# Attention and mixture of experts on one core: VectorE takes the lower halves of the expert weights, in four pieces per matrix

## The reference, cut to what matters

```python
scores_t = jnp.swapaxes(scores, 1, 2)
gate_vals, sel_idx = jax.lax.top_k(scores_t, capacity)        # capacity = 129
tokens = x[b_idx, sel_idx]
h = jnp.einsum('becd,edh->bech', tokens, w1) + b1[None, :, None, :]
h = jax.nn.gelu(h, approximate=False)
y = jnp.einsum('bech,ehd->becd', h, w2) + b2[None, :, None, :]
gated = y * gate_vals[..., None]
out = jnp.zeros_like(x).at[b_idx, sel_idx].add(gated)
```

## Time and profile before

| | us |
|---|---|
| median of 3 runs | 969.57 (967.61 to 969.59) |
| the profiled execution | 968.14 |
| its span, first to last instruction | 966.2 |
| TensorE busy with products | 833.6 (86% of the span) |
| VectorE, ScalarE, GpSimd busy | 649.0, 534.6, 527.7 |
| mean granted TensorE clock | 0.936 of full speed |

### The profile page before, as it was taken

The page is one execution under the profiler, slowest core; times in us unless marked ns, Lnnn a source line. Parts: engine busy times, 40 slices in busy tenths (PEclk is TensorE's granted clock), DMA queues, the critical chain, the costliest instruction groups (busy, mean ns, idle before and its releaser), DMA issues. The chain is left out here.

```text
span 966.2 us, 17052 instructions
## 1 busy us (share of the span) xinstructions
PE 833.6 (86%) x5864; PEld 623.9 (65%) x5864; DVE 649.0 (67%) x1985; ACT 534.6 (55%) x1042; POOL 527.7 (55%) x639
## 2 busy tenths in 40 slices
PE   4669999999999999977656899998989899898990
PEld 3434454544545453433356889998989899898990
DVE  4467778787877878999749955555464735547454
ACT  2126667667676766645345345564555556455455
POOL 6336665656565653323645247757375645738343
PEclk9768999999999999988879899999999999999995
DMA  4998778877776869100151324325242332422257
GB/s 142 165 151 134 123 121 144 144 144 143 141 147 112 153 99 205 62 24 20 47 202 53 74 40 82 96 38 137 35 126 45 93 63 47 125 34 35 37 132 250
DMA packets 90101, 100.51 MB, mean 104 GB/s; under 512 B 8736, under 2 KB 83488, under 8 KB 89888
## 3 DMA queue, kind: packets, MB, share of 16 engines
q1 hardware_dynamic: 72560, 77.92, 38.3%
q0 software_dynamic: 12800, 16.92, 10.3%
q10 hardware_dynamic: 4656, 4.59, 1.4%
HBM read 65.38 MB, written 33.62 MB: 102 GB/s over the span
## 5 line engine op out<-in xcount | busy, mean ns | idle before, releaser
L522 DVE CUSTOM_DVE_ANT_0 n_ps<-n_ps,tri 128x512 f32<-128x512 f32 (+3 forms) x512 | 238.8, 519 | 86.0 <-PE n_ps L652 84.3
L438 ACT ACTIVATE pt<-st_ps 128x512 f32<-128x512 f32 x320 | 184.3, 602 | 68.4 <-PE st_ps L637 53.2
L1090 DVE TENSOR_TENSOR h_lo<-g,h_hi 128x384 fp32r<-128x384 f32 (+1 forms) x184 | 132.6, 729 | 125.5 <-ACT h_hi L1026 116.3
L1166 PE MATMUL y_ps<-w_parts,h_hi 128*128 128x256 f32 (+1 forms) x1152 | 212.4, 279 | 0.3 <-ACT h_hi L1026 0.3
L1021 ACT ACTIVATE g<-h_ps,b 128x384 f32<-128x384 f32 (+1 forms) x192 | 104.3, 543 | 193.5 <-PE h_ps L1152 159.3
L1152 PE MATMUL h_ps<-tt_hi,w_parts 128*128 128x384 f32 (+1 forms) x768 | 177.3, 335 | 30.6 <-issue 20.0
L381 POOL TENSOR_SCALAR_AFFINE_SELECT pt<-pt 128x256 f32<-128x256 f32 (+1 forms) x320 | 110.7, 363 | 125.3 <-ACT pt L438 124.5
L1166 PEld LDWEIGHTS y_ps<-w_parts,h_hi 128*128 128x128 f32 (+1 forms) x1152 | 171.6, 177 | 3.6 <-ACT h_hi L1026 0.6
L993 POOL DMA_INDIRECT acc<-y,tok_no x64 | 103.7, 1621 | 114.7 <-DVE y L1104 105.9
L1166 PE MATMUL y_ps<-w_parts,h_lo 128*128 128x256 f32 (+1 forms) x576 | 160.6, 279 | 0.0
L1152 PEld LDWEIGHTS h_ps<-tt_hi,w_parts 128*128 128x128 f32 x768 | 132.2, 198 | 33.4 <-issue 31.8
(11 more groups left out here) (160 smaller groups left out, 1137.6 us busy)
## 6 DMA issues: line engine op xcount, KB each, us to landing
w_parts<-part_d SPq DMA_DIRECT2D x192, 128.0 KB, 6.5
w_raw<-in_w SPq DMA_DIRECT2D x16, 1024.0 KB
part_d<-w_raw SPq DMA_DIRECT2D x96, 128.0 KB, 6.6
w_raw<-in_xt SPq DMA_DIRECT2D x8, 512.0 KB, 4.7
res<-in_x SPq DMA_DIRECT2D x8, 512.0 KB, 10.4
x<-res SPq DMA_DIRECT2D x8, 512.0 KB, 3.3
acc<-res SPq DMA_DIRECT2D x8, 512.0 KB, 4.7
fin<-acc SPq DMA_DIRECT2D x4, 512.0 KB, 4.2
```

Source lines behind the costliest of these rows:

```text
L438: nc.scalar.activation(pt[:, slot % PT_RING, n % UP, :], st_ps[at % ST_RING][:, :], ACT.Exp, scale=S_SCALE).then_inc(exp_done, 1)
L522: ins = nc.vector.tensor_tensor_reduce(out=src[:, h, :], in0=src[:, h, :], in1=mask, scale=-1.0, scalar=-BIG_NEG, op0=ALU.add, op1=ALU.min ...
L1090: nc.vector.tensor_tensor(h_lo[:, q % 2, n, 0:cols], g[:, at % G_RING, 0:cols], h_hi[:, q % 2, n, 0:cols].bitcast(F32), ALU.subtract).then ...
L1166: ins = nc.tensor.matmul(y_ps[at % Y_RING][0:rows, 0:C], x[:, q % 2, m, toks], w[e % 2][:, m, :], start=i == 0, stop=i == len(terms) - 1)
```

## The change

In `experts`, GpSimd no longer makes the lower halves. VectorE makes each in four operations of 128 x 512, one per place of the order ("low1" and "low2", `low_at`): for experts 2 to 7 those of w1 at m = 3 to 6 of the pass of the cut, those of w2 at m = 7, 8, 9 and m = 0 of the next pass; for expert 1 those of w1 at m = 5 to 8 of pass 0, those of w2 at m = 9 of pass 0 and m = 0 to 2 of pass 1. A piece comes last at its place, behind "up", "turn" and "down". In `attention`, GpSimd still makes expert 0's, in four operations back to back. `w1_cut` and `w2_cut` count four per expert, and SyncE issues the next load at the stage of the fourth piece. ScalarE's part is as before.

```diff
@@ attention, gpsimd, stage "cut"
-                nc.gpsimd.tensor_tensor(lo, ahead[("w1_raw", "w2_raw")[n]][:, :, :], hi.bitcast(F32), ALU.subtract).then_inc(ahead[("w1_cut", "w2_cut")[n]], 1)
+                name, raw, cut = ("w1", "w2")[n], ahead[("w1_raw", "w2_raw")[n]], ahead[("w1_cut", "w2_cut")[n]]
+                for piece in range(PIECES):
+                    nc.gpsimd.tensor_tensor(piece_of(lo, name, piece), piece_of(raw, name, piece),
+                                            piece_of(hi, name, piece).bitcast(F32), ALU.subtract).then_inc(cut, 1)
@@
+PIECES = 4
@@
+def low_at(stage, e, piece):
+
+    q, m = cut_at("cut1" if stage == "low1" else "cut2", e)
+    m += (2 if stage == "low1" else 3 if e > 1 else 5) + piece
+    return q + m // (KH + 2), m % (KH + 2)
+
+
+def piece_of(part, name, piece):
+
+    if name == "w1":
+        return part[:, piece * KC // PIECES, (piece % 2) * HID // 2:(piece % 2 + 1) * HID // 2]
+    return part[:, piece * KH // PIECES:(piece + 1) * KH // PIECES, :]
@@ expert_steps, last at each place
+            for e in range(1, E):
+                for stage in ("low1", "low2"):
+                    for piece in range(PIECES):
+                        if (q, m) == low_at(stage, e, piece):
+                            yield stage, e, piece
@@ experts, sync
-            sp.wait_ge(w1_cut, e)
+            sp.wait_ge(w1_cut, PIECES * e)
...
-            if stage == "cut1" and q + 1 < E:
+            if stage == "low1" and n == PIECES - 1 and q + 1 < E:
                 load_w1(q + 1)
-            elif stage == "cut2" and q + 1 < E:
+            elif stage == "low2" and n == PIECES - 1 and q + 1 < E:
                 load_w2(q + 1)
@@ experts, gpsimd
-            elif stage in ("cut1", "cut2"):
-                raw, hi, lo, top, done = ((w1_raw, w1_hi, w1_lo, w1_top, w1_cut) if stage == "cut1" else
-                                          (w2_raw, w2_hi, w2_lo, w2_top, w2_cut))
-                pool.wait_ge(top, q + 1)
-                nc.gpsimd.tensor_tensor(lo[q % 2], raw[:, :, :], hi[q % 2].bitcast(F32), ALU.subtract).then_inc(done, 1)
@@ experts, vector
+            elif stage in ("low1", "low2"):
+                name, raw, hi, lo, top, done = (("w1", w1_raw, w1_hi, w1_lo, w1_top, w1_cut) if stage == "low1" else
+                                                ("w2", w2_raw, w2_hi, w2_lo, w2_top, w2_cut))
+                dve.wait_ge(top, q + 1)
+                nc.vector.tensor_tensor(piece_of(lo[q % 2], name, n), piece_of(raw, name, n),
+                                        piece_of(hi[q % 2], name, n).bitcast(F32), ALU.subtract).then_inc(done, 1)
@@ experts, tensor ("up" and, with w2_cut, "down")
-                    pe.wait_ge(w1_cut, e + 1)
+                    pe.wait_ge(w1_cut, PIECES * (e + 1))
```

More of the change, by code:

```diff
@@ L917, in load_w1 @@
         def load_w1(e):
-            sp.wait_ge(w1_cut, e)
+            sp.wait_ge(w1_cut, PIECES * e)
             sp.dma_start(w1_raw[:, :, :], w1_d[e].rearrange("(k p) n -> p k n", p=P)).then_inc(w1_in, 16)
         def load_w2(e):
-            sp.wait_ge(w2_cut, e)
+            sp.wait_ge(w2_cut, PIECES * e)
             sp.dma_start(w2_raw[:, :, :], w2_d[e].rearrange("(k p) n -> p k n", p=P)).then_inc(w2_in, 16)
@@ L939, in _ @@
                 if at >= FIN_OWN:
-                    sp.wait_ge(w1_cut, E)
-                    sp.wait_ge(w2_cut, E)
+                    sp.wait_ge(w1_cut, PIECES * E)
+                    sp.wait_ge(w2_cut, PIECES * E)
                 sp.dma_start(fin[at], acc_d[q * T:(q + 1) * T, :].rearrange("(t p) n -> p t n", p=P)).then_inc(fin_in[at], 16)
@@ L1159, in _ @@
                     pe.wait_ge(g_lo, KH * (q + 1))
-                    pe.wait_ge(w2_cut, e + 1)
+                    pe.wait_ge(w2_cut, PIECES * (e + 1))
                 if at >= Y_RING:
```

## The result

| | before | after |
|---|---|---|
| median, us | 968.59 (966.67 to 969.59, 4 runs) | 941.23 (938.76 to 941.67, 4 runs) |
| profiled execution, us | 968.14 | 940.88 |
| its span, us | 966.2 | 939.0 |
| GpSimd, VectorE busy, us | 527.7, 649.0 | 464.2, 623.4 |

A forecast was written before the change was run, and what follows sets the result against it. TensorE, 86% busy, was taken to stop before experts 2 to 7 because GpSimd's cuts hold VectorE up. 968.14 - 28.8 (idle and slow products) + 0.8 (first passes) + 0.3 (expert 2's w2) = 940.4, given as 941; range 936 to 951.

The forecast's parts named there:

- What holds VectorE: Experts' part: VectorE stands still until GpSimd's cut ends; all 14 cuts have a stretched VectorE instruction inside them.
- For the whole of GpSimd's operation: GpSimd and VectorE share SBUF interfaces: claimed that VectorE loses, for as long as GpSimd's operation lasts.
- The stops of experts 2 to 7: Six idle stretches of TensorE before each expert's first "up"; their removal gives back 18.5 us.
- the slow products behind the stops: First three "up" after each TensorE idle stretch, read as lower clock; 10.3 us to be recovered.
- A piece: One 128 x 512 subtraction on VectorE: takes 0.61 us of its time, lasts 0.69; 56 add 34 us.
- The first passes: Start of the experts' part, VectorE the bound: ends 0.8 us later, between 1 us earlier and 5 later.
- The new wait: Before job 2, TensorE waits for w1's fourth piece in place of tt_lo: starts 0.3 us later.
- Expert 2's w2: Pass 6: the fourth piece at m = 0 delays the first "down" by 0.3 us, between 0 and 0.7.
- The end of the attention: GpSimd's two operations become eight, 1.3 us more, covered by 1.44 us idle: costs nothing, 0 to 0.5 at risk.
- Late weights: Rival, chance 0.14: before each expert the fourth piece comes after TensorE is free; 960 us, at half of it 950.
- The slower case: Rival, chance 0.04: VectorE's long instructions wait for something else than GpSimd, the stops stay; 990 us.

## Why the prediction was right

**Sign and size.** 941 forecast, 941.23 measured; the profiled execution 940.4 forecast, 940.88 measured. Part of that closeness is luck: 1.65 us up to the first transposes, not forecast, went one way, and 1.7 us of slow products and 0.6 at expert 2 went the other.

**What holds VectorE.** Right, and shown: with a spare GpSimd operation on unrelated buffers the stuck instructions and the stops are back. The reading came from two lines of the timeline with the same end, not from the chain, which called the stops "issue". "For the whole of GpSimd's operation" does not hold in general: the spare one-input operation let h_lo go after 3.25 us, and four operations in a row held one instruction through all of them.

**The stops of experts 2 to 7.** Right: all six are gone. From expert 3 on 27.6 us were forecast and 27.62 measured, the slow products behind the stops included: these are gone where the stops are (granted clock 1.00 in each stretch of 50 us from 600 to 900).

**A piece.** 0.61 and 0.69 forecast; 0.60 apart and 0.683 measured. The formula of the Trainium skill, VectorE: DVE Perf Modes, section on the TRN2 errata, gives 0.691 for the length, and for 2048 columns 2.29 against 2.28 here. The same section advises tiles of 512 elements or more, and a piece has just 512. The trace agrees that each instruction pays anew (37.7 us of VectorE in 56 pieces, 31.9 in 14 operations), but that costs little time in this kernel: 4.3 of the 5.1 us between four pieces and one come from where the pieces stand, as the pieces set earlier show.

**The first passes.** The new wait was right: TensorE started job 2 later by 0.48 (forecast 0.3), ended by the piece and not by tt_lo. Job 3's start was put 0.8 late and came 0.62 late.

**Expert 2's w2.** The step "I put 0.3 us" was short: 0.68 idle, and the "down" behind it took 3.04 us in place of 2.80. It cost some 0.9, above the 0.7 that I had given as the upper bound. The fourth piece ended 3.55 us after the first "up" began, where the sum has 3.4, and the 0.25 us from there to the product were not in it.

**The end of the attention.** The 1.44 us for which GpSimd idled before the gathers were taken as slack. They were a wait for VectorE, which was itself stuck in the CAST of 2.17 us shown above. The outcome, nothing lost, was right, but not for that reason: GpSimd's eight operations took 9.86 us against 9.02, and the gathers still started 0.4 us sooner after the first of them. GpSimd's busy time fell by 63.5 us, where the prediction had some 68.

**What I did not see.** A loss of 1.7 us between job 3 and 606 us. After the third stop, for job 5's gathered tokens, TensorE ran slowly in the changed kernel and at full pace in the kernel before, though the stop is nearly as long (1.64 and 1.51 us). The granted clock and the products of the changed kernel there:

```profile
570.00:572.00 2.00, 2.00 (x10) 1.79 (x10) 0.86 (x2) 0.78 (x2) 1.70 (x2) 0.73 0.61 70
572.00:574.00 2.00, 2.00 (x11) 2.00 (x10) 0.14 (x1) 1.10 (x2) 1.57 (x2) 0.50 0.60 66
574.00:576.00 2.00, 2.00 (x17) 2.00 (x17) 0.41 (x1) 0.00 (x0) 1.52 (x2) 0.91 0.63 66
```

(Columns: stretch, length, then busy time and count of TensorE's products, its loads, VectorE, ScalarE and GpSimd, then the granted clock, the DMA share and GB/s.) The clock stands at 0.50, its lower level of 1.2 GHz, for a whole 2 us; before, the same stretches read 1.00. Both profiled executions of the changed kernel have the slow products (the second took 1.80 and 3.80 us for the products that take 1.25 and 2.80 at full clock). Of the four kernels with other places or one operation, two are slow after the second stop and two after the third. My sum took slow products away with the stops and did not ask whether those left would cost more.

**The rivals.** Late weights did not come true, and pieces at twice the price show by how little: 0.5 us of idle time per expert. The slower case, a hold by something else than GpSimd, is excluded: ScalarE's copies and the loads are still there in the changed kernel, and no instruction of VectorE is stuck.

## What to carry to other kernels

Look for instructions that last ten times their usual time and ask which other engine's instruction ends with them: a busy figure and the chain both hide that. Elementwise work over SBUF that GpSimd does "for free" can cost VectorE its whole length; count it as VectorE's time. Here it was then cheaper on VectorE itself (2.28 us for what took GpSimd 4.6 to 5.1). Where an operation moves into another engine's order, look at its place against the nearest deadline first: in this kernel that mattered more than whether it was cut small.

## What the runs showed of the hardware

- GpSimd's elementwise operation, of one input or two, held up VectorE's subtractions of two SBUF inputs (0.43 us turned into 4.15) and its SBUF-to-SBUF multiplication (0.35 into 5.48); a CAST from SBUF to SBUF took 2.17 us beside a cut of 2048 columns in the attention and 0.57 beside cuts of 512. The multiplication of 5.48 us and the one of 5.90 had each started 0.19 us ahead of GpSimd's operation by the profile, whose times for GpSimd are rough: being first did not spare them. The additions from PSUM took their 0.42 us beside it (660.04 above), and the token choice's MAX8, FIND_INDEX8 and MATCH_REPLACE8 their 0.67 to 0.69 beside the attention's cuts. The Trainium skill, GPSIMD Engine Reference, section 8, names VectorE's instructions with two SBUF inputs and those in a 2-port mode. The subtractions agree; no run shows in which mode the multiplication and the CAST, with one tensor as input, ran. That a one-input operation on GpSimd does it as well (988.43 us) I had not expected.
- Four GpSimd operations in a row can hold one VectorE instruction through all of them (5.90 us).
- GpSimd's operations are somewhat longer there too: 128 x 2048 took 4.51 us in the attention and 4.62 and 5.13 beside h_lo and the gate, 128 x 512 took 1.23 (eight in 9.86) and 1.37 (four in 5.49). That VectorE is the cause is not shown.
- On GpSimd the one-input operation was the slower: 5.64 us against 3.85 for two inputs, both 128 x 2048 in float32 and both read from b2. The subtraction of the weights, from two different buffers, took 4.87.
- How slow TensorE's products are after a short stop depends on more than that stop. At the wait for job 5's tokens 1.51, 1.56 and 1.66 us of idle time (before, pieces earlier, one operation) were followed by full pace, but 1.51 us with each piece done twice by a loss of 1.5 us and 1.64 in the changed kernel by 1.6; 2.42 and 2.29 in the two kernels with w2 behind tt_lo by 2.9 each. One stop earlier it is no different: 2.46 us (one operation) were followed by 4.93 us for 18 products, 2.67 (each piece twice) by 3.38. What decides it stays open.
